# The first products, the register loads and the last combines of a six-part transformer kernel, rearranged

## The reference

```python
x = x + 0.5 * _L0_ffn_ref(_layernorm(x), w_gate_up, w_proj)
x = x + _L0_attn_ref(_layernorm(x), w_qkv, w_out)              # 16 heads of 128
x = x + 0.5 * _L0_ffn_ref(_layernorm(x), w_gate_up, w_proj)
x = x + 0.5 * _L1_ffn_ref(_layernorm(x), gate_w, gate_b, ...)  # 8 experts and a shared one
x = x + _L1_attn_ref(_layernorm(x), W_Q, W_K, W_V)             # retention
x = x + 0.5 * _L1_ffn_ref(_layernorm(x), gate_w, gate_b, ...)

def _L0_ffn_ref(x, w_gate_up, w_proj):
    gate, up = jnp.split(x @ ternary_quant(w_gate_up).T, 2, axis=-1)
    return rms_norm(jax.nn.silu(gate) * up) @ ternary_quant(w_proj).T

def _L1_ffn_ref(xt, gate_w, gate_b, W1, W2, W3, Ws1, Ws2, Ws3):
    scores = jax.nn.softmax(xt @ gate_w.T)
    _, idx = jax.lax.top_k(scores + gate_b, 2)
    dw = ...                       # the scores of the two best experts of each token, else 0
    h = jax.nn.silu(xt @ W1[e].T) * (xt @ W3[e].T)             # for each expert e
    return sum_e dw[:, e] * (h @ W2[e].T) + jax.nn.silu(xt @ Ws1.T) * (xt @ Ws3.T) @ Ws2.T
```

## Time and profile before

| | us |
|---|---|
| median of three runs | 1614.95 |
| lowest and highest of them | 1613.34, 1616.31 |
| the execution that was profiled | 1613.27 |
| its span, first to last instruction | 1611.3 |
| TensorE busy | 1557.1 (97%) |
| VectorE busy | 1245.2 (77%) |
| ScalarE busy | 1214.3 (75%) |
| POOL busy | 1167.9 (72%) |

### The profile page before, as it was taken

How to read it: one execution, slowest core, us unless ns; L and a number is a source line. 1 busy time by engine, 2 the same in 40 slices (tenths; PEclk the granted TensorE clock), 3 DMA queues, 4 the chain that set the end, 5 groups by cost and what they waited for, 6 DMA issues and landing times. The chain is left out here.

```text
span 1611.3 us, 26807 instructions
## 1 busy us (share of the span) xinstructions
PE 1557.1 (97%) x9214; PEld 905.7 (56%) x9214; DVE 1245.2 (77%) x2324; ACT 1214.3 (75%) x1904; POOL 1167.9 (72%) x823
## 2 busy tenths in 40 slices
PE   3998899999999999999999999999999999999898
PEld 2566445555555555555555555555567566688575
DVE  7888777777777777777777778778888886988627
ACT  7876888989989998998898888887655543345442
POOL 0865888888888898888888888887575322476535
PEclk9999999999999999999999999999999999999999
DMA  9311879889779889879889887887401430000433
GB/s 310 128 54 41 141 140 170 144 144 180 150 151 168 155 153 168 158 144 169 164 146 165 152 159 142 159 153 137 84 1 33 129 83 4 1 1 8 107 98 98
DMA packets 641371, 197.10 MB, mean 122 GB/s; under 512 B 601547, under 2 KB 639062, under 8 KB 640982
## 3 DMA queue, kind: packets, MB, share of 16 engines
q1 hardware_dynamic: 636662, 188.19, 59.8%
q0 software_dynamic: 1536, 4.20, 0.8%
q10 hardware_dynamic: 3040, 3.02, 0.6%
HBM read 36.71 MB, written 10.22 MB: 29 GB/s over the span
## 5 line engine op out<-in xcount | busy, mean ns | idle before, releaser
L970 POOL TENSOR_TENSOR Pl<-Pm,Ph 128x1024 f16<-128x1024 f32 x256 | 545.9, 2132 | 43.8 <-ACT Ph L1311 43.5
L1301 ACT ACTIVATE Pm<-banks,nbias,s_scale 128x1024 f32<-128x1024 f32 x256 | 307.6, 1202 | 96.3 <-DVE nbias L1944 95.3
L1942 DVE TENSOR_REDUCE nmax<-banks 128x1 f32<-128x1024 f32 x256 | 311.7, 1218 | 88.3 <-PE banks L2517 87.8
L1311 ACT ACTIVATE Ph<-Pm 128x1024 f16<-128x1024 f32 x256 | 268.1, 1047 | 1.5
L949 POOL TENSOR_TENSOR rp_b<-rp_s,rope 128x512 f32<-128x512 f32 x128 | 163.1, 1274 | 98.7 <-ACT rp_s L1278 97.2
L1975 DVE SCALAR_TENSOR_TENSOR X<-banks,rinv,X 128x256 f32<-128x256 f32 x256 | 112.2, 478 | 113.0 <-PE banks L2517 113.0
L2515 PE MATMUL banks<-QK_hi 128*128 128x512 f16 x512 | 194.2, 379 | 1.6 <-DVE QK_lo L2033 0.9
L2516 PE MATMUL banks<-QK_lo,QK_hi 128*128 128x512 f16 x512 | 194.3, 379 | 0.0
L2517 PE MATMUL banks<-QK_hi,QK_lo 128*128 128x512 f16 x512 | 194.3, 379 | 0.0
L2515 PE MATMUL banks<-PT_hi,V_hi 128*128 128x512 f16 x512 | 194.0, 379 | 0.0
L2516 PE MATMUL banks<-PT_lo,V_hi 128*128 128x512 f16 x512 | 194.0, 379 | 0.0
(11 more groups left out here) (317 smaller groups left out, 3963.7 us busy)
## 6 DMA issues: line engine op xcount, KB each, us to landing
moe_raw<-in_L_ffn_W SPq DMA_DIRECT2D x48, 128.0 KB, 2.5
w_all<-in_L_attn_w_qkv SPq DMA_DIRECT2D x3, 2048.0 KB, 15.8
a_raw<-in_L_attn_w_qkv SPq DMA_DIRECT2D x24, 256.0 KB, 3.2
PT_hi<-Ph SPq DMA_TRANSPOSE x256, 3.4
PT_lo<-Pl SPq DMA_TRANSPOSE x256, 3.3
xs<-zeros SPq DMA_DIRECT2D x1, 2944.0 KB, 16.4
yd<-y_sb ACTq DMA_DIRECT2D x5, 512.0 KB, 2.9
raw_gu<-in_L_ffn_w_gate_up SPq DMA_DIRECT2D x2, 1024.0 KB, 7.3
```

What stands on the lines that cost most here:

```text
L970: nc.gpsimd.tensor_tensor(Pl[:, z % 4, :], Pm[:, k, :], Ph[:, z % 4, :], ALU.subtract).then_inc(pl_done.sem, 1)
L1301: nc.scalar.activation(Pm[:, k, :], two_banks[z % 2][:], ACT.Exp, bias=nbias[:, z:z + 1], scale=s_scale[:], accum_out=rsum[:, z:z + 1]).th ...
L1311: nc.scalar.activation(Ph[:, z % 4, :], Pm[:, (base * SLOTS + z) % 3, :], copy).then_inc(ph_done.sem, 1)
L1942: nc.vector.tensor_reduce(nmax[:, z:z + 1], two_banks[z % 2][:], AX, ALU.max, negate=True).then_inc(max_done.sem, 1)
```

## The change

Four things are changed.

- **Networks.** `MS_BANK` puts the sums of squares into bank 4 (bank 5 in one phase of f = 0). squares() waits for x_added only there, down products of odd j wait for ms_ready only there, and a product of the last phase that goes to bank 5 waits for x_added instead. The four normalisations at ht = 2 are split into two at ht = 2 and two at ht = 3. norm_guarded comes at ht = 3, ahead of the sums, and waits for a down product of the phase before.
- **Start of the last stage.** TensorE: up(0), up(1), turn(0), down(0), up(2), turn(1), down(1), logits, up(3). turn(1) uses banks 7 and 5. ScalarE puts hi(0) ahead of the fourth normalisation and silu(2) ahead of norm_hi(1). POOL puts bT_lo of unit 0 ahead of the second rstd. VectorE makes the first sums at i = 1 and the router's steps ahead of the product.
- **Registers.** `load_experts(g)` loads the four (or three) registers of a group at the head of up(i) of its unit.
- **Tail.** Combines come one unit sooner, the last two behind product(23); the gathers of tiles 0 and 1 stand both behind lo(15), the others one unit sooner.

The diff, cut to its core:

```diff
     ROUTER_AT, SCORES_AT, PICK_AT, WEIGHTS_AT = 3, 4, 5, 6
-    COMBINE_AT = {**{18 + t: (t,) for t in range(TT - 2)}, 16 + TT: (TT - 2, TT - 1)}
+    COMBINE_AT = {**{17 + t: (t,) for t in range(TT - 2)}, 15 + TT: (TT - 2, TT - 1)}
     SCATTER_BEHIND = {0: (2,), 1: (3, 4), 2: (5,), 3: (6, 7)}
-    GATHER_BEHIND = {15 + t: (t,) for t in range(TT)}
+    GATHER_BEHIND = {15: (0, 1), **{14 + t: (t,) for t in range(2, TT)}}
+    TURN_BANK = [(7, 6), (7, 5)]
     LO_BY_POOL = tuple(range(NUB))
...
     SQUARES_AFTER = 2
+    MS_BANK = [(4, 4, 5, 4), (4, 4, 4, 4)]
     POOL_LO = [[(1, 2, 4, 5, 6), (2, 4, 6), (2, 4, 6), (2, 4, 6)], [(2, 4, 6)] * 4]
...
                 scatter((1,))
-                rsqrt_ln(1, l, 1)
                 for i in LO_BY_POOL:
                     expert_lo(i)
+                    if i == 0:
+                        rsqrt_ln(1, l, 1)
                     scatter(SCATTER_BEHIND.get(i, ()))
...
 
-            def normalise(b, l, half):
+            def normalise(b, l, half, tiles=range(TPH)):
                 act.wait_ge(ln_shift.sem, SHIFTED.index((b, l, half)) + 1)
...
                     act.wait_ge(rows_lo.sem, half + 1)
-                for t in range(half * TPH, (half + 1) * TPH):
+                for t in (half * TPH + j for j in tiles):
                     nc.scalar.activation(XN[:, t, :], X[:, b, t, :], ACT.Identity, bias=shift[:, b, t:t + 1],
...
                     for c in range(DC):
-                        ln_hi_part(1, l, half, c, bank[7 - c])
+                        ln_hi_part(1, l, half, c, bank[TURN_BANK[half][c]])
 
                 silu(0)
-                normalise(1, l, 0)
+                normalise(1, l, 0, range(TPH - 1))
+                hi(0)
+                normalise(1, l, 0, (TPH - 1,))
                 silu(1)
-                hi(0)
                 norm_hi(0)
...
                 normalise(1, l, 1)
+                silu(2)
                 norm_hi(1)
-                for i in range(2, NUB):
+                hi(2)
+                for i in range(3, NUB):
                     if i > DOWN_LAG:
...
                 dve.wait_ge(w_norm_psum.sem, 1)
+                dve.wait_ge(down_ready.sem, down_ready.in_head(0, 2 * TPH + 1))
                 nc.vector.tensor_scalar(w_norm[:], bank[4][:, D:D + N_WEIGHTS], 1e-30, None, ALU.max).then_inc(w_norm_made.sem, 1)
...
                     tiles = slice(phase % NHALF * TPH, (phase % NHALF + 1) * TPH)
-                    nc.vector.tensor_scalar(ms4[:, tiles], bank[5][:, D:D + TPH], 4.0 / FF, 4 * RMS_EPS, ALU.mult, ALU.add).then_inc(ms_ready.sem, 1)
+                    nc.vector.tensor_scalar(ms4[:, tiles], bank[MS_BANK[f][phase]][:, D:D + TPH], 4.0 / FF, 4 * RMS_EPS, ALU.mult, ALU.add).then_inc(ms_ready.sem, 1)
 
...
                             mean_squares(phase - 1)
+                        if ht in (SQUARES_AFTER, SQUARES_AFTER + 1):
+                            tiles = range(2) if ht == SQUARES_AFTER else range(2, TPH)
                             if phase < 3:
-                                ln_normalise(1, l, phase - 1)
+                                ln_normalise(1, l, phase - 1, tiles)
                             else:
-                                ln_normalise(0, l + 1, 1)
+                                ln_normalise(0, l + 1, 1, tiles)
                         if ht in (4, 5, 7):
                             add(phase - 1, (4, 5, 7).index(ht))
-                        if (f, phase, ht) == (0, 3, 4):
-                            norm_guarded()
+                    if (f, phase, ht) == (0, 3, SQUARES_AFTER + 1):
+                        norm_guarded()
                     if phase > 1 and ht == 1:
...
                 for i in range(NUB):
-                    if i > DOWN_LAG:
+                    if i > DOWN_LAG + 1:
                         add(i - DOWN_LAG - 1)
-                    product(i)
-                    if i:
-                        lo(i - 1)
-                    if i == 0:
-                        shifts(1, l, 1)
-                    if i == 1:
-                        for half in range(NHALF):
-                            for c in range(DC):
-                                ln_lo_part(1, l, half, c, bank[7 - c])
-                            if half == 0:
-                                choice_weights(SORTED)
                     if i == ROUTER_AT:
...
                         last_weights(1)
+                    product(i)
+                    if i:
+                        lo(i - 1)
+                    if i == 1:
+                        ln_lo_part(1, l, 0, 0, bank[TURN_BANK[0][0]])
+                        shifts(1, l, 1)
+                        ln_lo_part(1, l, 0, 1, bank[TURN_BANK[0][1]])
+                        choice_weights(SORTED)
+                        add(0)
+                    if i == 2:
+                        for c in range(DC):
+                            ln_lo_part(1, l, 1, c, bank[TURN_BANK[1][c]])
                     for t in COMBINE_AT.get(i, ()):
...
                     pe.wait_ge(sq_added.sem, sq_added.in_head(f, (phase + 1) * (FT - 1)))
-                    if phase:
+                    if MS_BANK[f][phase] == 5:
                         pe.wait_ge(x_added.sem, x_added.before(0, l) + TPH * phase)
                     for j in range(TPH):
-                        last = nc.tensor.matmul(bank[5][:, D + j:D + j + 1], sq_sum[:, phase % NHALF, (FT - 1) % 2, j * P:(j + 1) * P], ones,
+                        last = nc.tensor.matmul(bank[MS_BANK[f][phase]][:, D + j:D + j + 1], sq_sum[:, phase % NHALF, (FT - 1) % 2, j * P:(j + 1) * P], ones,
                                                 start=True, stop=True)
...
                         pe.wait_ge(x_added.sem, x_added.before(0, l) + n - 1)
-                    if (END_BANKS[f][j] if phase == len(PHASES) - 1 else 4 + j % 2) == 5:
+                    if phase == len(PHASES) - 1 and END_BANKS[f][j] == 5:
+                        pe.wait_ge(x_added.sem, x_added.before(0, l) + TPH * phase)
+                    if MS_BANK[f][phase] == 5 and j % 2:
                         pe.wait_ge(ms_ready.sem, ms_ready.in_head(f, phase + 1))
...
 
-                def load_experts():
-
+                def load_experts(g):
+
+                    tiles = range(4 * g, 4 * g + GROUP_TILES[g])
                     pe.wait_ge(router_step.sem, routed(SORTED, N_BEST + N_SECOND + N_POSITIONS))
-                    registers = [nc.tensor.alloc_register(f"expert{j}") for j in range(SLOT_TILES)]
-                    nc.tensor.reg_load(registers, eid[:])
+                    registers = [nc.tensor.alloc_register(f"expert{j}") for j in tiles]
+                    nc.tensor.reg_load(registers, eid[:, tiles[0]:tiles[-1] + 1])
                     experts_of.extend(nc.s_assert_within(nc.tensor.snap(r), min_val=0, max_val=NE - 1,
...
                     if kind == "x":
+                        load_experts(g)
                         pe.wait_ge(xt_in[xt_set(g)].sem, 16 * len(XT_SETS[xt_set(g)]))
...
                     for c in range(DC):
-                        if half:
-                            pe.wait_ge(xT_done.sem, xT_done.at(1, l * LN_GROUPS + c + 1))
+                        if half and c == 0:
+                            pe.wait_ge(xT_done.sem, xT_done.at(1, l * LN_GROUPS + 1))
+                        elif half:
+                            pe.wait_ge(x_added.sem, added_by(0))
                         elif c == 0:
...
                             pe.wait_ge(x_added.sem, x_added.at(1, RET_X + TT - 1))
-                        transpose_part(1, l, half, c, bank[7 - c])
+                        transpose_part(1, l, half, c, bank[TURN_BANK[half][c]])
 
...
                 turn(0)
-                load_experts()
                 down(0)
+                up(2)
                 turn(1)
-                up(2)
+                down(1)
                 last_logits(DENSE)
-                down(1)
                 up(3)
```

## The result

The changed kernel takes 1618.07 us (median of 14 runs, 1616.89 to 1621.1), the kernel before 1614.78 us (14 runs, 1612.77 to 1616.31). The ratio is 1.0024, with a 95% interval of 1.0017 to 1.0031: +3.3 us where -1.8 was forecast, just outside the range.

The account below looks back on a forecast made before the run. TensorE, busy 1557.1 of 1611.3 us, was taken as the bound, so only closing its gaps or shortening the tail counts. Terms: −1.9 − 0.2 − 2.5 + 3.9 − 1.05 = −1.8, median about 1613.2 us, range 1610.0 to 1617.5.

Parts of the forecast that it names:

- Networks, -1.9: First network: TensorE's waits for ms (0.7), ff_h (0.64 of 1.1) and w_norm (0.57) go, −1.9 us.
- the 0.9 that I priced at 0: First network, squares' wait for X: it goes, but the gap is taken again at the attention behind VectorE's work, 0.
- the moves and the split add no instruction of length: Networks: moving and splitting operations lengthens no work, and ScalarE and POOL get their inputs no later.
- Second network, -0.2: Second network: one wait, 0.2 of the 0.7 left for ff_h, hangs on the same order and goes, −0.2 us.
- Start, -2.5: Start of the last stage: TensorE gains 3.3 by up(3), but POOL's chain and the first product by slots move 2.5.
- The cap of POOL: Start of the last stage: POOL's lo(3) can't begin before 1507.7, behind its scatter, so the chain moves by 2.5 at most.
- the fall of the clock that I took as cured: Behind down(0): granted clock 0.53 becomes near 1.00 with a gap of some 0.65, winning 1.3 + 0.3 us.
- Registers, +3.9: Units of slot tiles: five loads paid in full, 0.6 each plus 0.18 for register operation and dispatch, +3.9 us.
- Tail, -1.05: Tail: combines one unit sooner let product(25) start when TensorE is ready, at 1601.8, −1.05 us.
- a combine may wait up to 0.67 for one in time that is idle now: Tail: a combine's wait for its gather falls into VectorE's idle time, priced at 0.
- A slow clock that does reach the end, or a combine waits long: Rival: the longer read wait slows the clock to the end, or a combine awaits its gather; +3.5 and more, chance 0.05.
- The gains at the networks don't arrive: Rival: VectorE takes the networks' 1.9 back at the attention; sum +0.1, 1615.1 us, same; chance 0.14.

Follow-up runs that it names:

- e4_no_split3: The changed kernel with the four normalisations of each network's last phase together again: 1616.51 us against 1615.12 for the kernel before, ratio 1.0010.
- e1: The kernel before with six register loads, one heading each unit of slot tiles, instead of one of 23: 1617.2 us against 1615.12, ratio 1.0017.
- e6: The changed kernel with its six register loads two each ahead of down(2), down(3) and down(4): 1614.63 us against 1614.59 for the kernel before.
- f1_after_again: The changed kernel itself, profiled and timed again on a further chip: 1614.75 us against 1613.99 for the kernel before, ratio 1.0008.

## Why the prediction was wrong, point by point

- **Networks, -1.9: the size was right, one step wrong.** What I counted as gone went (e4_no_split3: -1.7 at the first scores, -1.5 counted from the first sums of squares), and the 0.9 that I priced at 0 was taken again as foreseen: in e4_no_split3 the sums of squares are 2.8 sooner and the first scores 1.7. The step that failed is "the moves and the split add no instruction of length". The earlier trace rows showed the price at 88 us, four normalisations in 3.30 us, and I used it only for where the split helps. I also put it down to ScalarE and POOL, and it is POOL alone. In the last phase the four had stood between two works of POOL, and the split moved two of them onto one: +1.4 for TensorE.
- **Second network, -0.2: wrong in sign, +1.1.** The 0.3 in the middle phases came; the +1.4 of the last phase is the same step as above, and in full, since nothing behind it takes it back.
- **Start, -2.5: right as a mechanism, and lost by what I had not priced.** The cap of POOL was right: on chips without gaps lo(3) stands right behind a scatter and unit 7 comes 28.2 us behind product(0), 2.9 sooner than in the profile that I read (1.9 against the kernel before on the same chip). The step that failed is that up(3) follows at full speed. I had the gap of 1.0 us in the logits before me as "issue" and put no row and no price on it; in the changed order, in the profile of the result, it is 1.55, and the fall of the clock that I took as cured came back behind it: up(3) 4.4 instead of 2.6 us. +0.5 instead of -2.5 in that pair of profiles.
- **Registers, +3.9: right as a mechanism, +3.2.** The reading of the earlier trace rows, that the sequencer sets the end, held in e1 and e6. The term was mis-sized by the load, which is 0.34 and not 0.6 for four of the groups, 0.78 for the last. The five make 2.1 us, and what is left of the 3.2 is 0.2 a unit for the register operation and dispatch, near the 0.18 taken. The rule of the Trainium skill ("Runtime: NRT & Kernel Launch", section "Instruction fetch mechanics"), 200 ns a register, would give 0.8 for four, an estimate; the trace disagrees for the loads of four, 0.33 to 0.52 us, and for the last, three registers in 0.78, from the other side. The floor of about 600 ns for a tensor load in the Trainium skill ("DMA: Bandwidth & Descriptors", section "Latency and other measured facts") isn't there: 327 ns is the shortest of all runs.
- **Tail, -1.05: -0.1.** The step that failed is "a combine may wait up to 0.67 for one in time that is idle now". It waits for the gathers of a pair of tiles, not of its own (both combines of a pair wait at one semaphore), and so runs into POOL's low part, behind which it ended; added to the four operations behind product(23), VectorE was 1.7 us behind at product(22), and my sum for product(25) had 0.4 to spare.
- **Rivals.** "A slow clock that does reach the end, or a combine waits long" (0.05) came nearest, and its +3.5 beside the measured +3.3 is luck. The combine's wait, with four operations behind product(23), cost the 1.0 that the tail didn't bring; the clock that it had in mind, behind the read, fell in seven profiles and cost nothing, and the one that cost fell behind the logits. "The gains at the networks don't arrive" (0.14) had the attention take them, which it did not. Three terms (networks, start, tail) each had one unpriced step, all on the same side; the registers were 0.7 too dear.

Sum as measured in the two profiles: -0.7 up to the last scores, +1.1, +0.5, +3.2, -0.1 = +4.0 of 4.1 us. The -0.7 is less than the attention's length varies. Luck has a part in the size of the miss too: on the chip of f1_after_again the changed kernel took 1614.75 us, inside the stated range, with the steps of the networks and the tail failed all the same.

## What to carry to other kernels

- Before moving an operation on VectorE, look at what POOL does at its new time, not only at who waits for it: a normalisation of 0.4 us took up to 1.7 when it started during a tensor operation of POOL, and a gap between two of these is worth keeping whole.
- A sequencer's instruction (a register load, a wait) costs what the sequencer is not ahead. Put it behind long matmuls that wait for nothing, never at the head of a stretch that the sequencer paces; the same six loads cost 3.2 us in one place and 0 in the other.
- A gap of TensorE with "issue" as its releaser among tiny matmuls is a term with a wide range, not a constant: it was 0 to 2.2 us between chips, and a fallen clock can hang on it. With long products of up(3) ahead of them, the logits had none.
- When a time hangs on such a term, one set of runs doesn't give the size of a small change: the same edit was +3.3 us in the result and +0.8 on a later chip.
